# Local attention in two stacks on one core: scores taken a slot later, norm spreads at the slot's end, the rotary addition first on GpSimd

## The reference

```python
def attn_layer(x, Wqkv, qs, ksc, Wo):              # 16 heads of 64
    q, k, v = split(x @ Wqkv)
    q = l2norm(q) * qs;  k = l2norm(k) * ksc
    q = q * cos * scale + rotate_half(q) * sin * scale
    k = k * cos / scale + rotate_half(k) * sin / scale
    sim = q . k over windows of 32 tokens, each sees itself and the 32 before
    out = softmax(sim * 8 + mask) @ v
    return out @ Wo
def ffn_layer(x, ...):                              # inner size 341, kept as 3 tiles of 128
    a, gate = split(layernorm(x) @ W1 + b1);  return a * gelu(gate) @ W2 + b2
for i in range(6):
    x = attn_layer(shift_tokens(x), ...) + x
    x = ffn_layer(shift_tokens(x), ...) + x
```

## Time and profile before

| what | value |
|---|---|
| time, median of 3 runs | 4340.56 us (4338.58 to 4354.18) |
| the profiled execution, its own time | 4352.9 us |
| its span, first to last instruction | 4351.2 us |
| granted TensorE clock, mean over the span | 0.959 |
| busy share PE, DVE, ACT, POOL | 93%, 77%, 71%, 41% |

### The profile page before, as it was taken

The page is one execution under the profiler, slowest core; times in us unless marked ns, Lnnn a source line. Parts: engine busy times, 40 slices in busy tenths (PEclk is TensorE's granted clock), DMA queues, the critical chain, the costliest instruction groups (busy, mean ns, idle before and its releaser), DMA issues. The chain is left out here.

```text
span 4351.2 us, 113662 instructions
## 1 busy us (share of the span) xinstructions
PE 4027.8 (93%) x43857; PEld 2388.8 (55%) x43857; DVE 3345.6 (77%) x4981; ACT 3100.0 (71%) x7032; POOL 1798.7 (41%) x1071
## 2 busy tenths in 40 slices
PE   7997999999999999999967689999999999999998
PEld 3443555555555555555536545555555555555554
DVE  5774888888888888888735478888888888888885
ACT  3555777777777777777762267777777778777776
POOL 3111444444444444444404534444444444444442
PEclk7997999999999999999986589999999999999999
DMA  2212444444443443444300044444434444444342
GB/s 44 31 21 70 95 111 102 99 101 101 105 111 90 111 107 90 111 99 103 84 10 3 3 107 109 101 97 109 110 87 115 102 100 100 102 105 111 92 100 52
DMA packets 232520, 380.78 MB, mean 88 GB/s; under 512 B 59364, under 2 KB 122336, under 8 KB 231688
## 3 DMA queue, kind: packets, MB, share of 16 engines
q1 hardware_dynamic: 231560, 372.20, 36.9%
q10 hardware_dynamic: 384, 0.79, 0.1%
HBM read 39.22 MB, written 1.05 MB: 9 GB/s over the span
## 5 line engine op out<-in xcount | busy, mean ns | idle before, releaser
L835 POOL TENSOR_TENSOR b_prob<-b_prob,b_rinv 128x768 f32<-128x768 f32 x384 | 564.3, 1469 | 1778.3 <-DVE b_rinv L1281 1778.3
L841 POOL TENSOR_TENSOR b_prc<-b_prc,b_sws 128x1024 f32<-128x1024 f32 x384 | 907.7, 2364 | 72.2 <-DMA b_sws<-b_prs 72.2
L1143 ACT ACTIVATE b_prob<-ps,b_nmx 128x96 f32<-128x96 f32 x3072 | 749.0, 363 | 0.0
L885 PEld LDWEIGHTS ps<-ident,b_prob 128*128 128x128 f32 x3072 | 367.9, 140 | 406.5 <-ACT b_pT L1079 232.8
L1216 DVE SCALAR_TENSOR_TENSOR b_prc<-ps,b_qks,b_rot 128x512 f32<-128x512 f32 x768 | 571.1, 744 | 14.0 <-ACT b_sq L1104 13.3
L1218 DVE SCALAR_TENSOR_TENSOR b_prs<-ps,b_qks,b_rot 128x512 f32<-128x512 f32 x768 | 570.1, 742 | 0.0
L885 PE MATMUL ps<-ident,b_prob 128*128 128x128 f32 x3072 | 513.0, 281 | 46.5 <-DVE b_kr L1264 37.1
L1262 DVE TENSOR_TENSOR b_prc<-b_prc,ps 128x512 f32<-128x512 f32 x384 | 263.6, 686 | 369.9 <-PE ps L950 288.3
L1079 ACT ACTIVATE b_pT<-ps 128x512 f32<-128x512 f32 x724 | 435.5, 601 | 154.1 <-PE ps L885 151.1
L987 PE MATMUL ps<-b_wqkv,b_xs 128*128 128x256 f32 x1536 | 435.0, 406 | 2.2 <-DVE b_prs L1218 2.2
L938 PE MATMUL ps<-b_xs,b_wqkv 128*128 128x512 f32 x768 | 408.9, 614 | 23.3 <-issue 10.0
(11 more groups left out here) (293 smaller groups left out, 7218.0 us busy)
## 6 DMA issues: line engine op xcount, KB each, us to landing
b_sws<-b_prs SPq DMA_DIRECT2D x1536, 128.0 KB, 2.3
b_vs<-b_va SPq DMA_DIRECT2D x384, 256.0 KB, 3.8
b_wqkv<-in_L_ffn_Wqkv SPq DMA_DIRECT2D x96, 192.0 KB, 3.6
b_xs<-y SPq DMA_DIRECT2D x126, 128.0 KB, 2.3
b_wo<-in_L_ffn_Wo SPq DMA_DIRECT2D x96, 64.0 KB, 3.1
b_xs<-y SPq DMA_DIRECT2D x42, 127.8 KB, 2.4
b_rot<-in_rot SPq DMA_DIRECT2D x2, 2048.0 KB, 7.8
b_w<-in_L_ffn_W SPq DMA_DIRECT2D x24, 170.5 KB
```

Source lines behind the costliest of these rows:

```text
L835: pool.tensor_tensor(prob[:, r, :, P - KEYS:P], prob[:, r, :, P - KEYS:P], rinv[:, r % 2, :].rearrange("p (b a) -> p b a", a=1).broadcast_ ...
L841: pool.tensor_tensor(prc[:, r, :, :], prc[:, r, :, :], sws[:, r % 2, :, :], ALU.add)\
L885: t = pe.transpose(bank[6][:, i * P:(i + 1) * P], prob[:, kd, 4 * e + 2 * h + m, :], ident[:, :])
L1143: g = act.activation(prob[:, kb, i, P - KEYS:P], wide[0][:, e * CH + m * KEYS:e * CH + (m + 1) * KEYS], ACT.Exp, bias=nmx[:, kb % 2, i:i + 1])
```

## The change

The same arithmetic is done in another order.

- TensorE: mask and scores now belong to `c_ = unit(3)`, and stand right behind `turn(.., 0)`, ahead of the K projection. Then come K, `turn(.., 1)`, the values projection, the strips (odd slots, into bank 3 where they were in bank 2), `values`, the two spreads of `b` (into banks 2 and 6 where they were in 2 and 3), then Wo. Wo waits for `ln_done` too in odd slots, since bank 3 holds the strips until then.
- ScalarE: the exponentials stand right behind the copy of the second turned half; behind them come the copy of the values projection, the copy `oT`, and in odd slots the three inverse-norm instructions.
- VectorE: maximum, split, K's products, sum and reciprocal, and at the slot's end the two multiplications by the spreads. A special copy of a turned half in one slot of six goes back to ScalarE.
- GpSimd: addition first, then product.

The diff, cut to its core:

```diff
@@ GpSimd @@
                     v, u = unit(1), unit(3)
+                    if v:
+                        U, r = um(v)
+                        pool.wait_ge(S["swap_ld"], ONE + 64 * (U + 1))
+                        pool.tensor_tensor(prc[:, r, :, :], prc[:, r, :, :], sws[:, r % 2, :, :], ALU.add)\
+                            .then_inc(S["add_done"], 1)
                     if u:
...
-                    if v:
...
@@ TensorE @@
-                def strips(U, b, pe=pe):
+                def strips(U, d, pe=pe):
                     pe.wait_ge(S["sqk_done"], ONE + U + 1)
-                    if b:
-                        pe.wait_ge(S["qn_done"], ONE + um(b)[0] + 1)
+                    if d:
+                        pe.wait_ge(S["y_add"], ONE + um(d)[0])
                     for s in range(4):
-                        m = pe.matmul(bank[2][32 * s:32 * s + 32, :], head_of[:, :], sq[:, s, :],
+                        m = pe.matmul(bank[3][32 * s:32 * s + 32, :], head_of[:, :], sq[:, s, :],
...
+                def spreads(b, d, pe=pe):
+                    UB, kb = um(b)
+                    pe.wait_ge(S["split_done"], ONE + twos(b) + 1)
+                    pe.wait_ge(S["kn_done"], ONE + UB)
+                    pe.matmul(bank[2][:, :], take[:, 2 * (kb % 2), :], rsp[:, :], start=True, stop=True)
+                    if d:
+                        pe.wait_ge(S["pt_cp"], ONE + 2 * um(d)[0] + 2)
+                    pe.matmul(bank[6], take[:, 2 * (kb % 2) + 1, :], rsp[:, :], start=True, stop=True).then_inc(S["nb_mm"], 1)
...
+                        turn(UD, kd, 0, c_)
+                    if c_:
+                        UC, kc = um(c_)
...
+                        mask(kc)
...
                     key_bank_free(f0)
                     if a:
                         pe.wait_ge(S["pk_done"], ONE + U)
                         pe.matmul(bank[1][:, :], W[:, 1, :], X, start=True, stop=True).then_inc(S["k_mm"], 1)
...
+                        turn(UD, kd, 1)
...
+                    if a and j % 2:
+                        strips(U, d)
+                    value_bank_free(f0)
+                    if d:
+                        values(d, 0)
+                        values(d, 1)
+                    if b:
+                        spreads(b, d)
                     if d:
...
                         pe.wait_ge(S["o_cp"], ONE + UD + 1)
...
                         pe.wait_ge(S["y_add"], ONE + UD)
+                        if a and j % 2:
+                            pe.wait_ge(S["ln_done"], ONE + twos(a) + 1)
                         pe.matmul(bank[3][:, :], wo[:, pair(d), :], oT[:, kd % 2, :], start=True, stop=True).then_inc(S["wo_mm"], 1)
@@ ScalarE @@
-                    if d and before != 5:
+                    if d:
                         turned(1)
...
                     if before == 5:
                         act.preload_act_table_set("natural_log_exp_and_others")
+                    if c_:
+                        UC, kc = um(c_)
+                        act.wait_ge(S["smax_done"], ONE + UC + 1)
...
                     if a:
                         act.wait_ge(S["va_mm"], ONE + U + 1)
...
-                    if a and j % 2 and before == 5:
+                    if step == 2:
+                        act.wait_ge(S["f_norm"], ONE + C + 1)
+                        act.activation(fin, fin, ACT.Identity, bias=lng[:, 1:2]).then_inc(S["f_in"], 1)
+                    if d:
+                        act.wait_ge(S["pv_mm"], ONE + 2 * UD + 2)
+                        act.activation(oT[:, kd % 2, :], bank[7], ACT.Copy).then_inc(S["o_cp"], 1)
+                    if a and j % 2:
                         inverse_norms(twos(a))
```

More of the change, by code:

```diff
@@ L940, in slot @@
                         UD, kd = um(d)
[L941 to L951, removed]
-                    if d and before != 5:
-                        turn(UD, kd, 0)
+                        turn(UD, kd, 0, c_)
+                    if c_:
+                        UC, kc = um(c_)
+                        if not d:
+                            scores_ready(UC)
+                        mask(kc)
+                        for m in range(4):
+                            for o, e in ((0, 0), (1, 1), (1, 0), (0, 1)):
+                                n = 2 * m + o
+                                at = PAD + (kc % 2) * CH + n * BLK - WIN
+                                es = slice(e * DH, (e + 1) * DH)
+                                g = pe.matmul(wide[0][o * BLK:(o + 1) * BLK, e * CH + m * KEYS:e * CH + (m + 1) * KEYS],
+                                              prc[es, kc, 0, n * BLK:(n + 1) * BLK], kr[es, at:at + KEYS],
+                                              start=False, stop=(m == 3), skip_group_check=True)
+                        g.then_inc(S["s_mm"], 1)
                     key_bank_free(f0)
@@ L957, in slot @@
                         pe.matmul(bank[1][:, :], W[:, 1, :], X, start=True, stop=True).then_inc(S["k_mm"], 1)
[L958 to L977, removed]
                     if d:
-                        values(d, 0)
-                        values(d, 1)
+                        turn(UD, kd, 1)
                     if a:
@@ L1084, in inverse_norms @@
                         act.wait_ge(S["split_done"], ONE + n)
-                        act.activation(rn[:, :], bank[2][:, :], ACT.Ln, bias=ss_eps[:, 0:1], scale=SS_SCALE)\
+                        act.activation(rn[:, :], bank[3][:, :], ACT.Ln, bias=ss_eps[:, 0:1], scale=SS_SCALE)\
                             .then_inc(S["ln_done"], 1)
@@ L1225, in slot @@
                     ok, OC = ffn_out(f0)
-                    follows = before in (0, 2, 4) or ok is not None
-                    if b and j % 2 == 0 and not follows:
-                        n = twos(b)
-                        dve.wait_ge(S["rn_done"], ONE + n + 1)
-                        dve.scalar_tensor_tensor(out=rsp[:, :], in0=rhi[:, :].bitcast(F32), scalar=minus_hi[:, 0:1], in1=rn[:, :],
-                                                 op0=ALU.mult, op1=ALU.add).then_inc(S["split_done"], 1)
                     if d:
@@ L1276, in slot @@
                         UC, kc = um(c_)
+                        sc = wide[0][:, :].rearrange("p (h c) -> p h c", h=2)[:, :, 0:4 * KEYS]\
+                            .rearrange("p h (i k) -> p h i k", k=KEYS)
+                        dve.wait_ge(S["s_mm"], ONE + UC + 1)
+                        dve.tensor_reduce(nmx[:, kc % 2, :], sc, AX.X, ALU.max, negate=True).then_inc(S["smax_done"], 1)
+                    if b and j % 2 == 0:
+                        n = twos(b)
+                        dve.wait_ge(S["rn_done"], ONE + n + 1)
+                        dve.scalar_tensor_tensor(out=rsp[:, :], in0=rhi[:, :].bitcast(F32), scalar=minus_hi[:, 0:1], in1=rn[:, :],
+                                                 op0=ALU.mult, op1=ALU.add).then_inc(S["split_done"], 1)
+                    if a:
+                        dve.wait_ge(S["sqk_done"], ONE + U + 1)
+                        products(U, r, a, 1, "pk_done")
+                    if c_:
                         dve.wait_ge(S["exp_done"], ONE + UC + 1)
```

103 lines of the change are left out of this document (35 added, 68 removed).

## The result

The changed kernel takes **4779.32 us** (median of 4 runs, 4778.14 to 4796.25) against 4339.57 us before (4338.48 to 4354.18): ratio **1.1014**, 95% interval 1.098 to 1.1048, so 10.1% slower. The prediction was 4748 us, slower with 92%, range 4560 to 4850. The profiled execution has a span of 4794.5 us, 443.3 more than the one before. One of the five runs of the first experiment took 7042.9 us, at a clock of 0.779, where the other four took 4315.91 to 4324.63; it is in no ratio.

The account below looks back on a forecast made before the run. TensorE bounds the kernel before; after, ScalarE's chain ahead of Wo. Per stack 96 x 8.62 + 96 x 9.21 + 208 + 11 + 31 = 1962 us against 1758, 407 more in both: 4748 us, range 4560 to 4850.

Parts of the forecast that it names:

- step 1: TensorE: the second turned half's wait for the first one's copy (232.8 us) goes; spreads move behind the values.
- step 2: TensorE: K, behind mask and scores, starts at 1.59 us, is charged 0.10 extra, and gives its result at 2.71.
- step 3: ScalarE: squares of K at 2.75 us, second turned half 3.29, exponentials 3.79, `oT` done at 6.68.
- step 4: Ahead of Wo, even slots: TensorE arrives at 5.4 us but waits for `oT` until 6.68; slot 8.62 instead of 7.10.
- step 7: FFN, per stack: matmuls add 208 us in full, one more ScalarE instruction 11, the exponential's table load behind gelu 31.
- Step 5: Odd slots: Wo also waits for the logarithm, which follows `oT` and ends at 7.27 us; slot 9.21 instead of 8.10.
- Step 6, the tie: Score ring: exponentials, sum, reciprocal and GpSimd's product end at 8.52 us, tying with the even slot's 8.62; nothing added.
- The lock: Rival: GpSimd's addition blocks VectorE's FFN product at step 2, up to 2.09 us each, 92 us in all: 4840; 7%.
- The clock: Rival: TensorE's waits lower its clock; a tenth of 3640 us at 1.2 GHz adds 218 us: 4966; 3%.
- the last sign of being wrong: TensorE: the prediction counts as wrong if the granted clock in a stack leaves 1.00.
- The sum: Whole stacks: 1962 us each against 1758, so 204 more per stack and 407 in both.
- the removed waits: TensorE's waits before the change: 91 us a stack, 182 in both, the most any new order can give back.

Follow-up runs that it names:

- the first experiment: Kernel before the change, with GpSimd's addition ahead of its product of the probabilities as the only edit: 4321.93 us, ratio 0.9952.
- experiment 6: Changed kernel with the strips in bank 1 (K's) and written behind the values: 4627.98 us, ratio 1.0654.
- experiment 7: Changed kernel with one exponential over 768 columns in place of eight, leaving out the subtraction of the maxima: 4569.98 us, ratio 1.0527.
- experiment 4: Changed kernel with the second spread done nine times in the slot behind each gelu, to fill TensorE's wait: 4763.79 us, ratio 1.0987.
- experiment 5: Kernel before the change, GpSimd's addition first except in slots where VectorE makes the FFN's norm product: 4318.54 us, ratio 0.9936.
- experiment 8: Changed kernel with GpSimd's order as before, product first and addition second: 4761.78 us, ratio 1.0975.

## Why the prediction was right, step by step

Steps 1 to 4 and 7 hold as mechanisms: the timelines show the chain of step 4 link by link, and experiments 6 and 7 take one part of it away each. The sizes, against the forecast's:

| from the turned half, even slot | forecast | measured |
|---|---|---|
| K starts | 1.59 | 1.48 |
| squares of K | 2.75 | 2.64 |
| exponentials | 3.79 | 3.61 |
| `oT` done | 6.68 | 6.55 |
| end of `oT` to the next turned half | 1.94 | 1.89 |
| even slot | 8.62 | 8.44 |
| odd slot | 9.21 | 9.17 |
| slot behind a gelu, step 0 of the next chunk (9.21 + 1.40 + four FFN matmuls of 0.86), Q to Q, undisturbed | 14.05 | 14.05 |

- Step 2 took 0.64 us from turned half to mask from the earlier trace rows; that row's 0.71 us held short pauses ahead of its second and fourth piece, 0.08 in all. In the changed kernel it is 0.53. The 0.10 that I charged to K behind the scores was right (1.12 in place of 1.02).
- Step 3: the second turned half's copy starts 0.49 behind the squares, not 0.54, since it no longer waits.
- Step 5 has the right time and the right last wait, but the wrong thing ahead of it. I had the logarithm behind exponentials and `oT`. In an odd slot `oT` waits for the values, and with a short exponential the slot stays at 9.17. Both paths come within 0.16 us of each other, so the number could not tell.
- Step 6, the tie, is right: GpSimd's product ends 0.09 ahead of the turned half, and binds as soon as the even slot is shortened (experiment 7).
- Two rivals came true in a few slots each, beside the forecast. The lock (7%): the norm product is blocked in all its 44 slots, by 0.15 us in the median and 1.55 at most. The clock (3%): 28 falls in the two loops, 99 us at the lower level, so at most 50 us; against the median of their kind the slots that it touched are 46 us longer. So the last sign of being wrong that the prediction names did come, in small: the granted clock over the loops is 0.99 and 0.98 (1.00 and 0.99 before, with 4 falls), not the tenth of the time at the lower level that the rival was worked out from. (That rival takes a tenth of 3640 us; the forecast's own stacks are 2 x 1962 = 3924, and with them it would be 4983.)

The sum: 407 forecast; even slots 192 x 0.18 = 35 less, odd ones some 10 less; the clock 46 more and the lock some 15 more (44 x 0.33, the mean of the product 1074 ns against 743). That makes 423, and 424 were measured in the loops. The 19 outside, mostly the longer draining of the pipelines, I had taken as nil. That the total came so near is in part luck: the slots were 45 us too long in the forecast, and the clock and the lock, which the sum put at nothing, gave 61 back.

What was given back by the removed waits can't be read as a time of its own: they were 91 us a stack in all, and the new wait took their place in nearly every slot. Nor does any run put back the old place of the spreads or the old order of VectorE alone, so what these parts of the change give or cost by themselves stays open.

## What to carry to other kernels

Before moving an operation forward in an engine's written order, list what stands behind it there and what the next engine does in the meantime. Here 1.8 us of exponentials moved ahead of a copy that TensorE needs, and TensorE had nearly nothing left to do at that point; in odd slots the strips moved ahead of the values and their reader, the logarithm, ahead of Wo, which by themselves make an odd slot as long. A chain through three engines is worked out well from the starts of neighbouring instructions in the trace; where two chains end within 0.2 us, only an experiment tells which one holds. A bank shared by two users adds the reader of one to the path of the other: moving the strips to another bank and behind the values gave 151 us, moving them to that bank alone nothing.

## What the runs showed of the hardware

- A VectorE instruction with two inputs in SBUF took 0.74 us alone and up to 2.83 us when GpSimd's addition had started first; it ended 0.55 us behind the addition (2645.74 against 2645.18, 4236.39 against 4235.84). The Trainium skill, SBUF — State Buffer, section "SBUF: two separate sides", has this as an exclusive lock; the traces agree, and experiments 1, 5 and 8 switch it on and off by the order on GpSimd alone.
- TensorE's granted clock fell to its lower level now and then inside the stacks. In the changed kernel's loops TensorE stood idle 57 times for 1.85 us or more at a stretch, and 27 of the 28 falls came just behind one; in the loops of experiment 6 there were two idle stretches over 1.5 us and one fall. Not every such stretch was followed by a fall, and where the wait was filled (experiment 4) none was left in those slots. What decides when it falls stays open.
